# Last stage of a two-layer graph kernel: the output product as f16 high and low parts, and the result added into the output by an accumulating DMA

## What is computed

```python
h = relu(layernorm(x))
x = x + GCN(h, edges)                       # "x1" of the kernel
h = relu(layernorm(x))
q, k, v = h @ Wq + bq, h @ Wk + bk, h @ Wv + bv
s = (q[row] * 32**-0.5 * k[col]).sum(per head)
a = softmax of s over the edges of each row
out = segment_sum(a * v[col], row)          # the "mean" of the kernel
return x + out @ Wo + bo                    # "result" = x1 + product
```

## Time and profile before

| | before |
|---|---|
| median of three runs | 3436.98 us |
| the profiled execution, its own time | 3437.03 us |
| its span, first to last instruction | 3435.2 us |
| mean granted clock of TensorE | 0.961 |
| PE busy over the span | 3089.9 us (90%) |
| DVE | 2812.0 us (82%) |
| ACT | 2503.3 us (73%) |
| POOL | 1953.9 us (57%) |

### The profile page before, as it was taken

The page is one execution under the profiler, slowest core; times in us unless marked ns, Lnnn a source line. Parts: engine busy times, 40 slices in busy tenths (PEclk is TensorE's granted clock), DMA queues, the critical chain, the costliest instruction groups (busy, mean ns, idle before and its releaser), DMA issues. The chain is left out here.

```text
span 3435.2 us, 80786 instructions
## 1 busy us (share of the span) xinstructions
PE 3089.9 (90%) x20244; PEld 2502.0 (73%) x20244; DVE 2812.0 (82%) x7373; ACT 2503.3 (73%) x7074; POOL 1953.9 (57%) x1668
## 2 busy tenths in 40 slices
PE   1699999699999569999999999994999999999999
PEld 0355555477776448888888888883899999999998
DVE  8788888578888358888888888885888888888887
ACT  0588888599997847777777777762777777777776
POOL 0344444045555277777777777763555555555553
PEclk6799999899999869999999999996999999999999
DMA  1355555388887658888888888875677777777774
GB/s 35 132 205 203 202 202 202 142 301 306 306 307 254 255 196 309 309 313 304 313 308 309 306 311 310 306 273 190 234 250 258 257 256 250 254 254 257 256 248 144
DMA packets 335629, 861.22 MB, mean 251 GB/s; under 512 B 98483, under 2 KB 152922, under 8 KB 323018
## 3 DMA queue, kind: packets, MB, share of 16 engines
q1 hardware_dynamic: 241082, 678.75, 55.2%
q0 software_dynamic: 66256, 78.94, 7.9%
q10 hardware_dynamic: 28224, 102.77, 7.4%
HBM read 521.95 MB, written 416.52 MB: 273 GB/s over the span
## 5 line engine op out<-in xcount | busy, mean ns | idle before, releaser
L1691 PE MATMUL c_qkv_ps<-w_qkv_hi,c_ht_hi 128*128 128x256 f16 x2352 | 642.0, 273 | 0.0
L1691 PE MATMUL c_qkv_ps<-w_qkv_lo,c_ht_hi 128*128 128x256 f16 x2352 | 642.0, 273 | 0.0
L1691 PE MATMUL c_qkv_ps<-w_qkv_hi,c_ht_lo 128*128 128x256 f16 x2352 | 642.0, 273 | 0.0
L2126 ACT ACTIVATE e_mine<-e_mine,e_attention 128x32 f32<-128x32 f32 x2352 | 518.7, 307 | 70.3 <-DVE e_attention L2360 70.3
L2073 POOL DMA_INDIRECT e_kv<-kv_table,e_near x392 | 402.1, 1026 | 113.1 <-issue 98.8
L1561 POOL DMA_INDIRECT c_got<-y_table,c_near x392 | 395.1, 1008 | 108.9 <-issue 98.0
L2162 PE MATMUL e_out_ps<-w_out,e_mean_t 128*128 128x256 f32 x1568 | 392.8, 380 | 0.0
L792 POOL DMA_INDIRECT dst_slots<-dst_word,dst_goal x240 | 236.9, 987 | 267.7 <-ACT a_hn L828 190.3
L862 PE MATMUL a_h_ps<-a_ht,w_t 128*128 128x512 f32 x784 | 361.1, 603 | 25.1 <-ACT h L810 21.5
L2065 POOL TENSOR_TENSOR e_kv<-e_kv,e_part_of 128x1024 f32<-128x1024 f32 x98 | 187.1, 1909 | 342.4 <-DVE e_part_of L2395 342.3
L1331 POOL DMA_INDIRECT src_slots<-staged_word,staged_goal x240 | 233.3, 972 | 250.8 <-DVE sort_lane_hot L1220 177.5
(11 more groups left out here) (432 smaller groups left out, 7682.2 us busy)
## 6 DMA issues: line engine op xcount, KB each, us to landing
kv_table<-c_kv SPq DMA_DIRECT2D x98, 1024.0 KB, 6.7
h_table<-h ACTq DMA_DIRECT2D x98, 512.0 KB
h<-h_table SPq DMA_DIRECT2D x98, 512.0 KB
y_table<-y_out ACTq DMA_DIRECT2D x98, 512.0 KB
agg_table<-agg_out SPq DMA_DIRECT2D x98, 512.0 KB, 3.2
c_agg<-agg_table SPq DMA_DIRECT2D x98, 512.0 KB, 5.6
x_table<-c_x SPq DMA_DIRECT2D x98, 512.0 KB, 2.9
q_table<-c_q SPq DMA_DIRECT2D x98, 512.0 KB, 4.3
```

Of the source, the lines that this page charges most:

```text
L1691: last = nc.tensor.matmul(qkv_ps[n][:, j * D:(j + 1) * D], h[u][:, kc, j * P:(j + 1) * P], wt[:, kc, n * D:(n + 1) * D], start=m == 0, sto ...
L2126: last = nc.scalar.activation(of_head, of_head, ACT.Copy, scale=attention[u][:, j, h, 0:1])
```

## The change

The output product and its result take another form, and the tensors that it needs are prepared elsewhere:

- w_out is split into w_out_hi and w_out_lo in f16, scaled by a power of two, and v is scaled too (unscale_v in place of unscale in stage C); the scales come from maxima that the setup takes with some DVE operations and one more all-reduce on POOL. The splitting itself and the preparation of b_out, eight operations that were in the setup, stand at the start of stage C.
- Stage C stores x1 into out, where it stored it into x1_table.
- ACT: `e_mean_hi`, f16, takes the place of `e_mean_t`; in front of each of the two stands a new `more<-out_ps,out_unscale`, the product times the scale back, for the tile that lags by 4.
- DVE: result is gone; in its two places of the step stands `low`, mean_lo = mean_ps - mean_hi in f16, for the tile that lags by 3.
- PE: a row of the product is the bias and six f16 matmuls (hi·hi, hi·lo, lo·hi for both kc) in place of the bias and two f32 ones (each of which the trace shows as two). A half waits for both mean_lo.
- SP: neither loads x1 nor stores the result. POOL adds `more` to out behind the four gathers of the step by a DMA with accumulation, after both halves of more are there; more[w] is a ring of 3.

```diff
@@ gpsimd, last stage
-                over_ring(pool, NT, 2, 3, step)
+                    if at(4) is not None:
+                        t, (w, n) = ring_tile(at(4)), in_ring(at(4), SHORT)
+                        hold(pool, result_ready, t * 2 + 2)
+                        if isinstance(t, int) and t == NT - 1:
+                            pool.dma_start(out[t * TILE:plan.n, :].rearrange("(p r) d -> p (r d)", r=ROWS),
+                                           flat(more[w][0:plan.last_p, :, :]), accum_op=ALU.add).then_inc(stored[w], 16)
+                        else:
+                            pool.dma_start(row_block(out, t), flat(more[w][:, :, :]), accum_op=ALU.add).then_inc(stored[w], 16)
+
+                over_ring(pool, NT, 2, 4, step)
+                for w in short:
+                    pool.wait_ge(stored[w], 16 * len(range(w, NT, SHORT)))
@@ scalar
                     for kc in range(KC):
+                        if at(4) is not None:
+                            t, (w, n) = ring_tile(at(4)), in_ring(at(4), SHORT)
+                            if kc == 0 and (not isinstance(n, int) or n > 0):
+                                hold(act, stored[w], n * 16)
+                            act.wait_ge(product_ready, t * 2 + (kc + 1))
+                            nc.scalar.activation(more[w][:, kc * 2:kc * 2 + 2, :], out_ps[:, :, :], ACT.Copy,
+                                                 scale=out_unscale[:, 0:1]).then_inc(result_ready, 1)
                         if at(3) is not None:
                             t, u = ring_tile(at(3)), at(3)[1] % 2
                             wait_past(act, product_ready, (t - 2) * 2 + 2)
                             act.wait_ge(mean_ready, t * 2 + (kc + 1))
-                            nc.scalar.activation(mean_t[u][:, kc, :], mean_ps[kc][:, :], ACT.Copy).then_inc(mean_t_ready, 1)
+                            nc.scalar.activation(mean_hi[u][:, kc, :], mean_ps[kc][:, :], ACT.Copy).then_inc(mean_hi_ready, 1)
@@ tensor
-                    pe.wait_ge(mean_t_ready, t * 2 + 2)
+                    pe.wait_ge(mean_lo_ready, t * 2 + 2)
                     wait_past(pe, result_ready, t * 2 + half)
...
-                        for kc in range(KC):
-                            last = nc.tensor.matmul(out_ps[:, j, :], mean_t[u][:, kc, row * P:(row + 1) * P],
-                                                    w_out[:, kc, :], start=False, stop=kc == KC - 1)
+                        passes = [(m, w, kc) for kc in range(KC)
+                                  for m, w in ((mean_hi, w_out_hi), (mean_hi, w_out_lo), (mean_lo, w_out_hi))]
+                        for k, (m, w, kc) in enumerate(passes):
+                            last = nc.tensor.matmul(out_ps[:, j, :], m[u][:, kc, row * P:(row + 1) * P],
+                                                    w[:, kc, :], start=False, stop=k == len(passes) - 1)
@@ vector
-                def result(at, half):
...
-                    v.tensor_tensor(here, out_ps[:, :, :], here, ALU.add).then_inc(result_ready, 1)
+                def low(at, kc):
+                    t, u = ring_tile(at), at[1] % 2
+                    dve.wait_ge(mean_hi_ready, t * 2 + (kc + 1))
+                    wait_past(dve, product_ready, (t - 2) * 2 + 2)
+                    v.tensor_tensor(mean_lo[u][:, kc, :], mean_ps[kc][:, :], mean_hi[u][:, kc, :], ALU.subtract).then_inc(mean_lo_ready, 1)
@@ vector, step
                         products(at(1))
-                    if at(4) is not None:
-                        result(at(4), 0)
+                    if at(3) is not None:
+                        low(at(3), 0)
                     if at(2) is not None:
                         normalise(at(2))
...
                         parts(at(2))
-                    if at(4) is not None:
-                        result(at(4), 1)
+                    if at(3) is not None:
+                        low(at(3), 1)
@@ vector, start of stage C
+                v.tensor_scalar(b_out_n[:, :], b_out_n[:, :], both_scale[:, 0:1], None, ALU.mult)
+                chain(v.tensor_scalar(w_flat, w_flat, out_scale[:, 0:1], None, ALU.mult))
+                chain(v.tensor_copy(w_out_hi[:, :, :], w_out[:, :, :]))
+                chain(v.tensor_tensor(w_out_lo[:, :, :], w_out[:, :, :], w_out_hi[:, :, :], ALU.subtract))
```

More of the change, by code:

```diff
@@ L272, in build @@
         unscale = sb("unscale", [P, 1], where=early)
+        unscale_v = sb("unscale_v", [P, 1], where=early)
+        out_scale = sb("out_scale", [P, 1], where=early)
+        both_scale = sb("both_scale", [P, 1], where=early)
+        w_out = sb("w_out", [P, KC, D], where=early)
+        b_out_n = sb("b_out_n", [P, D], where=early)
         b_qkv = sb("b_qkv", [P, 3 * D], where=early)
@@ L971, in build @@
             y_stored = [sem(f"y_stored{u}") for u in two]
-            agg_stored = [pool_dma_sem(f"agg_stored{u}") for u in two]
+            agg_stored = [sem(f"agg_stored{u}") for u in two]
             own_scale = sb("own_scale", [P, NT * ROWS], where=part)
@@ L1459, in build @@
             not_slow = sb("c_not_slow", [P, 1], where=part)
+            b_rest = sb("b_rest", [P, 2, D], where=part)
+            b_thirds = sb("b_thirds", [P, 3, D], BF16, where=part)
             slots_loaded = sem("c_slots_loaded")
@@ L1507, in step @@
                         hold(sp, x1_ready, tile + 1)
-                        sp.dma_start(row_block(x1_table, tile), x1[u][:, :, :].rearrange("p r d -> p (r d)")).then_inc(x1_stored[u], 16)
+                        if isinstance(tile, int) and tile == NT - 1:
+                            sp.dma_start(out[tile * TILE:plan.n, :].rearrange("(p r) d -> p (r d)", r=ROWS),
+                                         x1[u][0:plan.last_p, :, :].rearrange("p r d -> p (r d)")).then_inc(x1_stored[u], 16)
+                        else:
+                            sp.dma_start(row_block(out, tile), x1[u][:, :, :].rearrange("p r d -> p (r d)")).then_inc(x1_stored[u], 16)
                     if at(9) is not None:
@@ L1912, in build @@
             q = [sb(f"e_q{w}", [P, ROWS, D], where=part) for w in short]
-            x1 = [sb(f"e_x1_{w}", [P, ROWS, D], where=part) for w in long]
+            more = [sb(f"e_more{w}", [P, ROWS, D], where=part) for w in short]
             near = [sb(f"e_near{w}", [P, ROWS], I32, where=part) for w in long]
@@ L1931, in build @@
             part_of = [sb(f"e_part_of{w}", [P, ROWS, H], where=part) for w in short]
-            mean_t = [sb(f"e_mean_t{u}", [P, KC, TILE], where=part) for u in two]
+            mean_hi = [sb(f"e_mean_hi{u}", [P, KC, TILE], F16, where=part) for u in two]
+            mean_lo = [sb(f"e_mean_lo{u}", [P, KC, TILE], F16, where=part) for u in two]
             turn_ps = part.enter_context(nc.psum_tensor("e_turn_ps", [P, ROWS, 2 * P], F16))
@@ L1948, in build @@
             q_loaded = [sem(f"e_q_loaded{w}") for w in short]
-            x1_loaded = [sem(f"e_x1_loaded{w}") for w in long]
-            stored = [sem(f"e_stored{w}") for w in long]
+            stored = [pool_dma_sem(f"e_stored{w}") for w in short]
             near_ready = sem("e_near_ready")
@@ L2018, in step @@
                             sp.dma_start(flat(q[w][:, :, :]), row_block(q_table, t)).then_inc(q_loaded[w], 16)
-                    if at(0) is not None:
-                        t, (w, n) = ring_tile(at(0)), in_ring(at(0), RING)
-                        wait_past(sp, stored[w], n * 16)
-                        if not isinstance(t, int) or t >= SHORT:
-                            sp.dma_start(flat(x1[w][:, :, :]), row_block(x1_table, t)).then_inc(x1_loaded[w], 16)
-                    if at(4) is not None:
-                        t, (w, n) = ring_tile(at(4)), in_ring(at(4), RING)
-                        sp.wait_ge(result_ready, t * 2 + 2)
-                        if isinstance(t, int) and t == NT - 1:
-                            sp.dma_start(out[t * TILE:plan.n, :].rearrange("(p r) d -> p (r d)", r=ROWS),
-                                         flat(x1[w][0:plan.last_p, :, :])).then_inc(stored[w], 16)
-                        else:
-                            sp.dma_start(row_block(out, t), flat(x1[w][:, :, :])).then_inc(stored[w], 16)
                 over_ring(sp, NT, 2, 4, step)
-                for w in long:
-                    sp.wait_ge(stored[w], 16 * len(range(w, NT, RING)))
             @block.gpsimd
```

71 lines of the change are left out of this document (47 added, 24 removed).

## The result

The changed kernel takes **3683.53 us** (median of 4 runs, 3679.78 to 3687.29) against 3437.47 us of the kernel before: a ratio of 1.0715, 95% interval 1.07 to 1.0731, or +246 us. The direction was forecast, the size was not: +95 us were expected, and the range ended at 3590.

What follows compares the result with a forecast made beforehand. PE was taken to bound the last stage (10.41 us a tile), and after the change a ring of 11.35 us through four engines. 3437.03 + 88 (ring) + 2 (setup) + 5 (end) = 3532 us, range 3500 to 3590.

Steps and rivals of the forecast that it cites:

- it decides only above X = 1.28: Last stage, ring through POOL's issue and share: 10.07 + X us a tile, hidden with 0.26 us to spare.
- X: Time of POOL's accumulating issue per tile: 0.87 us and 0.15 of hand-over, taken as 1.02.
- the ring of 11.35: Last stage, all four engines through mean_hi, attention, 16 products and second mean_lo: 11.35 us a tile against 10.41, +88 us.
- PE's product: Last stage, half an output product on PE: 1.53 us against 1.94, saving 0.82 us a tile.
- That a wait closes at the first mean_lo: Last stage, DVE's first mean_lo waits for ACT's mean_hi: starts 3.70 us after the product's start, break-even 2.83.
- the second ring: Last stage, product to attention 6.02, hand-over 0.05, PE's edge matmuls to next product 5.18: 11.25 us a tile.
- rival B: Accumulating issue is dear: at X = 2.0 12.07 us a tile, 3600 us; far end 8.45, 4220 us; chance 0.09.
- rival C: PE's clock falls because it now idles in every last-stage tile: 3606 us, chance 0.05.
- Rival A: Faster: the subtraction mean_lo doesn't wait and DVE binds the last stage: 3401 us, chance 0.09.
- DVE's 9.95: Last stage, DVE's need per tile, hand-overs included: 10.41 less its one real wait of 0.46 us.
- Setup and start of C: Setup: +2 us (bounds 0 and +5); start of stage C: twelve new DVE operations hidden in its idle time, 0.
- The end: Last tile's end and drain: +2.6 for more, issue and landing, about +2 for longer order; +5 us (bounds 0 and +10).

Runs made afterwards that it cites:

- e2: Changed kernel with the first mean_lo moved behind normalise on VectorE, nothing else: 1.0255 of the kernel before, +92 us.
- e9: Changed kernel with ScalarE's loop shifted and POOL's accumulating issue a step later, ahead of the gathers: 1.0537 of the kernel before, +185 us.
- e1: Changed kernel with 40 one-column copies ahead of ScalarE's last-stage loop, shifting its code: 1.0536 of the kernel before, +186 us.
- e14: Changed kernel with 10 one-column copies ahead of ScalarE's last-stage loop: 1.0705 of the kernel before, +240 us.
- e5: Changed kernel with mean_lo behind normalise, ScalarE's loop shifted, POOL's issue a step later and ahead of the gathers: 1.0001 of the kernel before.
- e10: Changed kernel with mean_lo behind normalise, ScalarE's loop shifted, POOL's DMA plain (x1 not added): 1.0035 of the kernel before, +12 us.
- e7: Changed kernel with mean_lo behind normalise, ScalarE's loop shifted, SP storing plainly for POOL (x1 not added): 0.9986 of the kernel before, -5 us.

## Why the prediction was right or wrong

Three steps failed: that of POOL, "it decides only above X = 1.28", with X taken as 1.02 where the tile gives 2.11; the ring of 11.35, which left out a path; and the code loads, which weren't in the sum.

- **PE's product**: right. A half takes 1.53 us (2973.97 to 2975.50), as summed:

```profile
2973.97 0.27 PE L2206 MATMUL e_out_ps<-b_out,all_b 128*128 128x256 bf16 x1
...
2975.50 0.60 PE L2220 MATMUL e_mean_ps<-ident,e_mine 128*128 128x128 f32 x4
```

- **That a wait closes at the first mean_lo**: right in place and sign. e2 alone takes 154 of the 246 us away.
- **The length of that ring**, 11.35: wrong, because a path was left out. I followed attention to ScalarE and to PE's edge matmuls, and in the second ring took the 5.18 from the edge matmuls to the next product as PE's work alone. In e9 it is 5.76 (2812.57 to 2818.33), for the seen matmuls in it wait for DVE's own work behind attention, up to e_of_edge. By that path a tile takes 11.7 to 11.9 (e9), where the clock is 1.00.
- **POOL**, "it decides only above X = 1.28", X = 1.02: here the term was mis-sized. In the form of my sum, 10.07 + X, the tile of 12.18 gives X = 2.11. From the end of more to the start of share are 1.39 us: 0.75 until the issue starts (I had 0.15), then 0.64 of the issue, which takes 1.00 where I had 0.87. Share, which starts under it, takes 0.41 more. And from share's end to mean_hi are 1.40 for 1.14, which I had as unchanged: e_below is held by share, and so are the exponential, the first more and mean_hi. 1.02 + 0.37 + 0.41 + 0.26 and 0.05 of small ones are 2.11. So rival B, with a chance of 0.09, was the steady state, and its price for X = 2.0, 12.07, came close; but its reason was only part of it, as three small terms made X, and the dear issue of its far end, 8.45, didn't come.
- **Code**: not in the prediction in any form. I counted 22 more instructions a turn on ScalarE at nothing. They are 48 to 60 us of the 246 (e1, e14), with the first mean_lo in place. In the kernel after that is more than the stalls by themselves: a turn is 4.9 us longer for 2.75 to 3.45 of stall. The tiles behind a stall have a lower clock, which fits the rest.
- **The clock**, rival C: partly. It is 0.95 in the stage; 28 of 84 tiles have 0.77 to 0.96, among them those of 13.0 to 13.15 us behind a stall, with 0.87. In e1, without the code stalls, all 84 have 1.00 and quiet tiles are 12.2 just the same, so the clock isn't the cause of 12.2. In e9 it costs some 53 us.
- **Together**: 151 us came on top of the forecast. (12.18 - 11.35) x 94 = 78 of them are the quiet tile, 48 to 60 the code loads with the clock behind them; the rest, 13 to 25 us, wasn't followed.
- **Rival A**, 3401, rested on DVE's 9.95: wrong also by its own terms. With the first mean_lo and the issue out of the way (e5) the time is 3436, for 0.46 of those 10.41 us are a ring.
- **Setup and start of C**: +2 was forecast; the last stage starts 7.7 us earlier than before (PE's first turn matmuls at 2370.62 for 2378.34) and 6.2 of these come from the start of stage C, as told below. The stage itself grew by 253 us. The end was forecast at +5; from the last attention to the end of the kernel are 28.2 us for 21.3, +6.9.

## What to carry to other kernels

Where engines run in-order programs against each other, follow a new wait out of every engine that it reaches, the waiting engine's own later work too, until it comes back: the longest of these rings is the period, and an idle time inside one is no slack. An operation of VectorE with two operands from SBUF that meets one of GpSimd on SBUF counts as a dependency (e_below and share here), though no semaphore shows it. Before two runs are compared, look at the granted clock tile by tile: a shorter ring and a lower clock can cancel, as in e9. And count the instructions that are added to a loop body: the queue that loads code, one line of the page, tells whether it is loaded again in each turn.

## Hardware behaviour that was not expected

**GpSimd's DMA issues beside VectorE.** The 8.45 us scatter of the earlier trace rows takes 1.62 us in the changed kernel, in which twelve short operations have pushed the DVE group of 7.1 us back; now a plain gather that meets the group takes 7.05 us for about 1.0. POOL, then DVE:

```profile
1197.70 1.62 POOL L1390 DMA_INDIRECT agg_table<-sum_summed,sum_goal  x1 [8.84 <-ACT sum_summed L1606]
...
1204.49 7.05 POOL L1590 DMA_INDIRECT c_got<-y_table,c_near  x1 [0.31 <-issue]
```

```profile
1204.28 7.14 DVE L1822 TENSOR_SCALAR absent<-own_degree 128x392 bf16<-128x392 f32 x8
```

The gather ends at 1211.54, the group at 1211.42. So the length is DVE's, whichever issue it meets. The Trainium skill, page "SBUF — State Buffer", section "SBUF: two separate sides", says that descriptors of a DMA issued from GpSimd can't be written while DVE runs an operation in a mode that takes the ports the two engines share; the two issues agree with it. And the first of stage C's results comes at 1217.94 for 1224.15.

**An accumulating DMA** costs POOL 1.00 us to issue for 0.58 of a plain one of the same 512 KB (e10), and lands 7.4 us (median) after its issue, where the plain one of e10 takes 6.2 and SP's plain store of the same tensor in e7 takes 2.9, as in the earlier trace rows. So most of the longer landing goes with the queue and not with the accumulation.
